# The sort of a graph network's edges: chunks of seven static steps, and one-hots as comparisons with one column each

## The reference

```python
edge_index = jnp.stack([src, dst])
x = _layernorm(x + _L0_gnn_ref(x, src, dst, edge_type_8, ...))
x = _layernorm(x + _L1_gnn_ref(x, edge_attr_16, ..., src, dst, 12500))
x = _layernorm(x + _L2_gnn_ref(x, ..., edge_index, edge_type_8))
x = _layernorm(x + _L3_gnn_ref(x, edge_index, ...))
```

## Time and profile before

| | us |
|---|---|
| median of 3 runs | 16641.76 |
| lowest and highest | 16610.89, 16656.3 |
| the profiled execution, its span | 16996.1 |
| busy in it: PE | 11995.3 (71%) |
| DVE | 10824.2 (64%) |
| ACT | 8088.7 (48%) |
| POOL | 5158.9 (30%) |
| idle of DVE ahead of L953, over all | 2428.1 |

### The profile page before, as it was taken

How to read it: one execution, slowest core, us unless ns; L and a number is a source line. 1 busy time by engine, 2 the same in 40 slices (tenths; PEclk the granted TensorE clock), 3 DMA queues, 4 the chain that set the end, 5 groups by cost and what they waited for, 6 DMA issues and landing times. The chain is left out here.

```text
span 16996.1 us, 429738 instructions
## 1 busy us (share of the span) xinstructions
PE 11995.3 (71%) x146289; PEld 8312.1 (49%) x146290; DVE 10824.2 (64%) x19718; ACT 8088.7 (48%) x16130; POOL 5158.9 (30%) x4771
## 2 busy tenths in 40 slices
PE   1343443434434344799799998997996999999998
PEld 0111111111111111466688886665664888888887
DVE  3233333333333333688788887887886899999998
ACT  1232433433424234566466664665664555555554
POOL 1656666565664656000111111000000111111111
PEclk8555555555555555899899998999998999999999
DMA  7122222222222222688222222887885222333322
GB/s 208 48 72 59 81 67 66 81 59 71 74 58 79 58 72 82 184 229 229 89 106 106 106 106 95 234 235 198 235 235 126 80 83 83 85 85 84 84 84 71
DMA packets 1721891, 1905.31 MB, mean 112 GB/s; under 512 B 981549, under 2 KB 1429103, under 8 KB 1696207
## 3 DMA queue, kind: packets, MB, share of 16 engines
q1 hardware_dynamic: 1602775, 1863.79, 37.0%
q0 software_dynamic: 116864, 39.75, 1.5%
q10 hardware_dynamic: 2078, 0.15, 0.0%
HBM read 1449.57 MB, written 453.42 MB: 112 GB/s over the span
## 5 line engine op out<-in xcount | busy, mean ns | idle before, releaser
L688 POOL DMA_INDIRECT rec<-sort_ring,sort_idx x3520 | 4042.6, 1148 | 2791.9 <-issue 1469.7
L1381 DVE TENSOR_TENSOR e_full<-e_feats,e_masks 128x3840 bf16<-128x3840 bf16 x1179 | 2523.7, 2154 | 350.5 <-ACT e_feats L1339 302.0
L1294 PE MATMUL e_acc<-e_full,e_sel 128*128 128x384 bf16 (+1 forms) x11760 | 2120.9, 327 | 270.4 <-DVE e_full L1381 270.2
L778 PE MATMUL sort_ps_count<-sort_hot,upper_b 128*128 x400 | 231.6, 579 | 2689.9 <-DVE sort_hot L903 2144.6
L1530 PE MATMUL e_acc<-e_outer,e_sel 128*128 128x272 f32 x7840 | 1896.8, 397 | 3.9 <-DVE e_outer L1625 3.9
L1337 ACT CAST e_masks<-e_kind 128x1280 bf16<-128x1280 fp8e4 x1179 | 1482.6, 1258 | 629.5 <-DVE e_full L1381 575.0
L731 ACT CAST sort_cols_t<-sort_ps_late 120x256 f16<-120x256 f32 x98 | 39.5, 403 | 3439.8 <-remote 2373.0
L1530 PEld LDWEIGHTS e_acc<-e_outer,e_sel 128*128 128x128 f32 x7840 | 1459.2, 190 | 281.2 <-issue 4.1
L953 DVE TENSOR_TENSOR sort_over<-sort_ps_late,sort_late_base 128x20 f32<-128x20 f32 x175 | 30.7, 176 | 2428.1 <-remote 2208.7
L1294 PEld LDWEIGHTS e_acc<-e_full,e_sel 128*128 128x128 fp8e4 x11760 | 1061.0, 97 | 933.2 <-issue 298.1
L751 ACT ACTIVATE sort_made<-sort_ps_count,sort_window_bias 128x1024 fp8e4<-128x1024 f32 (+1 forms) x1274 | 1378.7, 1156 | 71.9 <-remote 26.7
(11 more groups left out here) (463 smaller groups left out, 22855.8 us busy)
## 6 DMA issues: line engine op xcount, KB each, us to landing
e_hot<-stream SPq DMA_DIRECT2D x888, 480.0 KB, 3.8
stream<-sort_made SPq DMA_DIRECT2D x98, 2568.0 KB
e_sel<-stream SPq DMA_DIRECT2D x1176, 160.0 KB, 2.7
e_st<-stream SPq DMA_DIRECT2D x99, 1888.0 KB, 7.3
sheaf_gather<-stream SPq DMA_DIRECT2D x393, 384.0 KB, 3.1
e_hot<-stream SPq DMA_DIRECT2D x294, 448.0 KB, 3.5
tail<-sort_made SPq DMA_DIRECT2D x98, 660.0 KB
sheaf_by_dst<-tail SPq DMA_DIRECT2D x491, 128.0 KB, 3.0
```

The lines of the kernel that those rows point to most:

```text
L688: nc.gpsimd.indirect_dma_start(out=rec[q], out_offset=bass.IndirectOffsetOnAxis(ap=idx[:, s, q, c:c + 1], axis=0), in_=ring[:, s, q, c, :] ...
L1294: last = mm(acc[h][:, 0:cols_all], now[:, n * P:(n + 1) * P], full[q & 1][:, n, :], start=j == 0, stop=j == NT - 1)
L1381: v.tensor_tensor(full[q & 1][:, :, 0:cols].rearrange("p j (t k f) -> p j t k f", t=TYPES, k=3), feats[q & 1][:, :, :, :].unsqueeze(2).to_ ...
```

## The change

The steps are taken by chunks of seven, and all places within a chunk are constants of the program. `quad_chunks` counts chunks of 35 tiles a block; with these inputs each quad is one chunk, so 175 steps remain. The ring has two sides instead of 8 places, one chunk each. SP loads a chunk's attributes with 4 DMAs of 128 x 735 elements (35 tiles x 21), 2940 bytes to a partition in one piece; for that the host lays `attr` out as [partition, tile, 21] with room for the fields. These loads overwrite the fields' room, so ACT's copies now wait for them, and ACT also writes the column of ones. ACT makes the keys of a chunk in 4 ops of 35 columns and the fields in one op of 128 x 140 and 4 of 128 x 35 x 4. DVE waits for keys and ring once a chunk, POOL for the fields once a chunk and for `idx` at each step. The steps of pads are gone on all engines. In the build, the two ops of L987 become 15 comparisons of the row 0 to 97 and 15 of the row 0 to 127 with one source column each, and L1017 becomes 40 comparisons of the row 0 to 127 with one column of a new f32 tile, `dst_lo`, each; the sources are f32 too. Rows and windows of the second half move to partitions 32 to 34, with a second set of windows made at the start.

```diff
-RING = 8
+STEPS = 7
+CT = STEPS * C
...
-        ring = sb("ring", [P, RING, Q, C, RW])
-        idx = sb("idx", [P, RING, Q, C], I32)
-        keys = sb("keys", [P, RING, Q, C])
+        ring = sb("ring", [P, 2, Q, CT, RW])
+        idx = sb("idx", [P, 2, STEPS, Q, C], I32)
+        keys = sb("keys", [P, 2, Q, CT])
...
                         for q in range(Q):
-                            sp.dma_start(ring[:, place_of(i), q, :, 0:D].squeeze(1),
-                                         edges[:, tiles(t0[q] + local(i, i0) * C, C), :]).then_inc(attr_in, 16)
+                            sp.dma_start(ring[:, side_of(i), q, :, :].squeeze(1), attr[:, chunk_tiles(t0[q], i, i0), :])\
+                                .then_inc(attr_in, 16)
...
+                def scatter(side, chunk, rounds, first):
+
+                    pool.wait_ge(fields_ready, chunk + 1)
+                    pool.sem_inc(passed, 1)
+                    for s in range(STEPS):
+                        pool.wait_ge(idx_ready, chunk * STEPS + (s + 1))
                         pool.sem_inc(passed, 1)
                         for c in range(C):
                             at = s * C + c
...
                     with act.Fori(i0, i1) as i:
                         act.wait_ge(scattered, i + 1)
-                        nc.scalar.copy(ring[:, place_of(i), 0, :, D + 1:D + 5].squeeze(1), e.fields[:, 0:C, :]).then_inc(fields_ready, 1)
+                        act.sem_inc(act_passed, 1)
+                        for q in range(Q):
+                            last = nc.scalar.activation(keys[:, side_of(i), q, :].squeeze(1), e.key[:, chunk_tiles(t0[q], i, i0)],
+                                                        ACT.Identity, bias=key_bias[:, bass.ds(n, 1), q:q + 1].squeeze(1))
+                        last.then_inc(keys_ready, 1)
+                        act.wait_ge(attr_in, i * (16 * Q) + 16 * Q)
+                        act.sem_inc(act_passed, 1)
+                        nc.scalar.copy(ring[:, side_of(i), :, :, D:D + 1].squeeze(1).squeeze(3), ones)
+                        for q in range(Q):
+                            last = nc.scalar.copy(ring[:, side_of(i), q, :, D + 1:D + 5].squeeze(1),
+                                                  e.fields[:, chunk_tiles(t0[q], i, i0), :])
+                        last.then_inc(fields_ready, 1)
...
-                    find(i0, n)
                     with dve.Fori(i0, i1) as i:
-                        find(i + 1, n)
-                        place(i, n)
-                    dve.sem_inc(taken, 1)
+                        a = i * STEPS
+                        dve.wait_ge(keys_ready, i + 1)
+                        dve.wait_ge(scattered, i + 1)
+                        dve.sem_inc(dve_passed, 1)
+                        find(i, a, 0)
+                        for s in range(STEPS):
+                            if s + 1 < STEPS:
+                                find(i, a, s + 1)
+                            place(i, a, s)
...
-                        shape = [P, SORT_SHARE, w]
-                        last = v.tensor_tensor(out[h], sources[:, h, k, :].unsqueeze(2).to_broadcast(shape),
-                                               m.iota[:, 0:w].unsqueeze(1).to_broadcast(shape), ALU.is_equal, saturate=False)
+                        for t in range(SORT_SHARE):
+                            last = v.tensor_scalar(out[h][:, t, :], m.iota[:, 0:w], sources[:, h, k, t:t + 1], None, ALU.is_equal,
+                                                   saturate=False)
...
-                    v.tensor_tensor(now[:, ST_SEL:ST_KIND].rearrange("p (j n) -> p j n", n=P),
-                                    m.iota_b[:, :].unsqueeze(1).to_broadcast([P, NT, P]),
-                                    cols[:, h, 1, 2, :].unsqueeze(2).to_broadcast([P, NT, P]), ALU.is_equal, saturate=False)\
-                        .then_inc(kinds_made, 1)
+                    dve.wait_ge(lo_made, b + 1)
+                    dve.sem_inc(dve_passed, 1)
+                    for j in range(NT):
+                        last = v.tensor_scalar(now[:, ST_SEL + j * P:ST_SEL + (j + 1) * P], m.iota[:, :], dst_lo[:, h, j:j + 1], None,
+                                               ALU.is_equal, saturate=False)
+                    last.then_inc(kinds_made, 1)
...
-                i0, i1 = all_steps(dve)
-                with dve.Fori(i0, i1) as i:
-                    dve.wait_ge(scattered, i + 1)
-                    v.tensor_copy(idx[:, place_of(i), :, :].squeeze(1), none[:, :, :])\
-                        .then_inc(idx_ready, 1)
...
-    host["attr"] = np.pad(attr, ((0, ATTR_TILES * P - N_EDGES), (0, 0)))
+    host["attr"] = np.ascontiguousarray(attr.reshape(ATTR_TILES, P, RW).transpose(1, 0, 2))
```

## The result

The changed kernel took 17432.7 us (median of 4 runs, 17408.0 to 17472.2) against 16649.0 of the kernel before (4 runs, 16610.9 to 16661.3): a ratio of 1.046, 95% interval 1.0429 to 1.0491. It is slower by 784 us, where I forecast 234 us less. As the experiments then showed, this holds on some chips; on others the same kernel is faster by 3.1%.

The account below looks back on a forecast made before the run. The sort was taken as bound by a chain between engines, none full. 24 x (-11.4 - 3.0 + 1.0 + 4.0) = -226, with +6 - 14, gave -234: about 16410 us, 8-in-10 range 15900 to 16890.

Parts of the forecast that it names:

- The bound and the late news: Sort stage: no engine is full; a chain bounds it, and PE's counts reach DVE late while POOL issues scatters without a pause.
- The steps: Seven index steps of a quad in the sort: predicted to fall from 139.4 to 128 us, -11.4 us a quad.
- step 4 is released when POOL has run through the 80 scatters: Sort's index steps: the fifth index waits for POOL's scatters of the first four steps and 6 us more, 111 us.
- Rival B: Attribute loads cause the late news: seven steps take about 50 us, POOL's pace bounds, -57 us a quad, 15270 us; 12%.
- What the steps give: Sort's period: the steps' -11.4 us a quad was counted in full over 24 quads.
- Static addresses: DVE's register work between index and next search goes, about 0.6 us a step; with waits once per quad, -3.0 us a quad.
- One-hots: Build of the blocks: three large DVE ops become 70 small ones, 11.7 us against 9.3, hidden behind ACT: 0.
- the lost relief: Build: without POOL's pauses at long one-hots, PE results reach ACT late; +4.0 us a quad, between 0 and 17.
- quad 3: Profiled sort period with a slow build, 137.1 instead of 120.4 us, where a PE result reached ACT 5.21 us late.
- rival D: Slower: the build loses its relief, +17 to 24 us a quad, +80 to +250 us in all, 16720 to 16890; 25%.
- The setup and the end: Sort's start and finish: +6 us for small DVE ops and ring clearing, -14 us for the dropped step of pads.
- The sum: Whole kernel: 24 quads' terms, -226, with +6 and -14 give -234 us, taken off the median 16641.8 us.

## Why the prediction was wrong

- **The bound and the late news**: right. L953's waits come from POOL's issuing: with a pause each round they fall from 2489.7 to 1.9 us on one late chip.
- **The steps**: the direction was right and the size was off. The term was -11.4 us a quad; measured -62.6 (139.4 to 76.8) between the two traces, and -42.0 (141.3 to 99.3) with the chunks alone on one chip. The step that failed was "step 4 is released when POOL has run through the 80 scatters". In quad 7 the longest wait at L953 was 11.44 us and none went on until POOL ran dry; in 17 of the 25 quads no wait reached 25 us, and the other eight have one of 36 to 44. Rival B (about 50 us) was nearer. Which side of the attribute loads did it is open.
- **What the steps give**: the sum took 24 times the steps' gain off the time and let the build stay as it was. That failed too. With the chunks alone 32 of the 42 us came back in the build of the same chip (125.6 to 157.5), since more of the build then falls into POOL's run.
- **Static addresses**: 6.95 to 6.14 us a step, 0.8 instead of 0.6.
- **One-hots**: here the prediction broke. "0.17 each: 70 make 11.7 us" came from a row of a later stage in which POOL does not scatter; beside POOL on a late chip they started 0.7 to 2.1 us apart. And the lost relief was priced at +4.0 a quad, with 17 from quad 3 as its upper bound; the build rose by 82 us, of which the chunks alone make some 30. Quad 3 was no bound, since in it a long operation still came and the gaps behind it were gone. My own rival D said that, and had the place and the sign; it was sized at +80 to +250 us instead of +784.
- **The setup and the end**: the first index comes 5.3 us later, with +6 forecast. From the last index to the last one-hot of the sort it is 260.0 us instead of 164.9, so the end rose by 95 where I forecast -14: the build beside POOL's last run is late as well. Whether the 14 us of the pads are in it can't be told apart.
- **The sum**: between the two traces +5 for the setup, +439 for the 24 periods, -64 for the last quad's steps and +95 for the end make +475, against +474 between the spans (17470.3 and 16996.1). The rest of the 784 is that the runs of before (16649) and its trace (16996) did not take the same time. I had written that the sort's waits are no part of what separates these two. But in all 20 traces of this case the part behind the sort takes 10084 to 10171 us, so at least some 290 of these 347 us lie in the sort. That it is the late news, stronger in the one than in the other, is likely and not shown.
- **Rival B's sum** has a slip: 262.8 less 203 is 60 a quad, not 57, which gives about 15210. It changes no chance.
- **What none of my cases held**: that the whole mechanism depends on the chip. On a quiet chip the changed kernel gains 496 us, by what I had written off as worth nothing by itself: POOL is spared its pauses, and there POOL is the bound. That this makes the whole 496 us is worked out, as said above, and not shown.
- **The two rules of the Trainium skill.** "SBUF — State Buffer" ("Who interferes with whom") says that `tensor_scalar` can enter a mode that locks GpSimd out. Here it did not: beside 70 of them a block a scatter took 981 ns in the mean on a late chip and 1005 on a quiet one, against 1148 and 1069 beside `tensor_tensor`. The same section also says that an instruction with two inputs in SBUF contends with a GpSimd instruction that reads SBUF, which I had left out of the prediction; L1017 has two, and its 5.61 us scatter agrees. "VectorE: DVE Perf Modes" asks for large tiles for the sake of the fixed latency. On the quiet chip 40 tiles of 128 took 8.1 to 8.2 us, against 5.48 for one of 5120 in the trace of before; so small tiles do cost more, and it is hidden there, since POOL is the bound. What made them costly on the late chip was neither rule.

## What to carry to other kernels

A long operation that blocks another engine can be what keeps the rest of a chain alive: before it is split, look at what its pause relieved. One long operation left in place need not be enough, as the kernel with the selection long shows (17427 against 17433 us), and a deliberate pause has its price: each round, it took the delays away and gained nothing over the kernel before (17081 against 17061). A gain in one half of a period counts only if the other half stays as it was; look at the period. Take the price of a small instruction from rows in which the same neighbours run, since beside uninterrupted scatters the same comparisons started 0.7 to 2.1 us apart instead of 0.2. When a trace and the timed runs differ by 2%, do not take it to cancel; look for the term that differs, and if at all possible see both kernels on more than one chip.

## What the hardware showed beyond this

Chips of one type differed by 5 to 8% on the same program (15740 against 16610 and 17061), and the change was 3.1% faster on one of the quick ones and 4.6% slower on a slow one; each was met once. On a late chip, beside scatters 1.27 us apart, starts of instructions on DVE and answers between PE and ACT fell on multiples of about 0.70 us; the state outlasted POOL's last scatter by 13 to 16 us, in most of which no DMA moved. Waits of 2.0 to 2.3 us ahead of each four scatters kept it from arising. A pause of 5.5 us ended it in 19 of 27 cases with all one-hots long, and in 1 of 33 among short ones. Why the news is late, no view shows.
